# A two-direction state-space scan: half of the state sum by an accumulating transfer, row squares in four column groups

## Chip, cores and metric

The kernel runs on one core of a Trainium2 chip. The metric is the time of one execution on the device, in microseconds (us); lower is better. TensorE does the matmuls, VectorE and ScalarE the elementwise work, POOL (GpSimd) some elementwise work and the transfers that add into their destination, SP (SyncE) the plain transfers.

## What is computed

Tokens are looked up in a table, a two-direction Mamba block is added, then an attention block and a mixture of experts. Only the Mamba block is touched. Cut to what matters:

```
def step(h, ins):
    dt_t, B_t, C_t, u_t = ins
    dA = exp(dt_t[..., None] * A)
    h = dA * h + (dt_t * u_t)[..., None] * B_t[:, None, :]
    return h, einsum('bdn,bn->bd', h, C_t)
...
dt = softplus(x_dbl[..., :DT_RANK] @ Wdt.T + bdt)
y = (scan(step) + uc * Dp) * silu(z)
out = layernorm(y @ Wout.T)             # once forward, once on the reversed rows
combined = concat([fo, bo]) @ Wfuse.T + bfuse
```

32 sequences of 512 rows with 256 channels; inside, 512 channels and 32 states.

## The kernel before

One call, `mamba_stage`, walks through 64 **slots**: for each sequence s a forward one (d = 0) and a reverse one (d = 1), t = 2 s + d. Channels lie on partitions, in four tiles of 128, each 512 rows long; work on two tiles at once (128x1024) is called a half. Five engines run loops written by hand (each `slots`), in a fixed order, tied together by semaphores. A slot finishes the scan of t and at the same time prepares t + 1, and it carries the layer norm and the fusion of t - 1.

VectorE, in order: `conv` of t + 1 (L834), `dead_part` (L899, the states that have decayed, into qq), `scan` (L889, the live state, into tp), in the reverse slot `ln_stats`, `bc_product` (L842), `outputs` (L904: tp times C, 128x2048 in one operation), `more_states` (a branch that is not taken here), in the forward slot `xt_low` (L821), `sums` (L942: tp plus qq, two halves), `gate` (L951: tp times silu(z) into yz, two halves), `dead_test` (L851, L853), `softplus` of t + 1 (L874 and L877 for each half), `dead_mask`, `softplus_end` (L882, writes v, from which the next slot's scan inputs and decays start).

ScalarE, ahead of softplus: v (L448), abs (L457), in the forward slot `xt_copy` (L410), exp, sum (L474), `row_var` (L396, the mean square of a row of t - 1, plus eps), log (L480), `finish` (L510: the fused rows scaled into fb), then `last_tap_and_bias` (L420) for the next convolution and the decays (L485).

TensorE: z projection of t + 1 (L641; waits for the convolution), x_dbl (L650), first half of the fusion (L712), dt projection (L659), second half, `row_squares` (L701: the squares as weights, a column of ones moving, eight matmuls, two records each), u projection (L641), `dead_sums` (L666) in the middle of it, `dead_count`, `out_proj` of t (L690; waits for finish on ScalarE, whose PSUM it overwrites, and for the gate), `state_sum` (L682) in the middle of that.

POOL: `add_input` (L337, transfers that add uc times D into qq), `add_rows` (L316, transfers that add fb into the result), forward `add_bias` (L305), reverse `ln_scale` (L285 to L290), `row_scale` (L297: the root that finish waits for), forward `gather` of sequence s + 2 (L274, L277, four indirect transfers), `scan_inputs` (L322, L328).

Of the kernel before, what the change touches and what calls it, by code (L numbers as in the profile page):

```python
# [56 lines left out]
def mamba_stage(nc, tok_ids, table, w, h1_dram):  # L57
# [6 lines left out]
    with ctx:  # L64
# [3 lines left out]
        def sem(name):  # L68
# [55 lines left out]
        r2 = sb("r2", [P, TT])  # L124
        r3 = sb("r3", [P, TT])
# [19 lines left out]
          d0_ok dt_ok dtu_ok tp_ok da_ok h_ok hc_ok q_ok du_ok mix0 mix1 yv_ok yz_ok xm_ok qd_ps gt_ok ct_ok cnt_ps  # L145
          fl_ok s_ps o_ps fo_ok sq_ok ss_ps rv_ok rr_ok f_ps fin_ok h1_st acc gt2 e_bc e_da e_tp e_h e_hc e_y""".split()
# [44 lines left out]
        def _(sp):  # L191
# [3 lines left out]
            def broadcast(t, d):  # L195

                if not (isinstance(t, int) and t < 2):
                    wait_apart(sp, S["hc_ok"], t - 1)
# [10 lines left out]
            def more_states(t, d):  # L209
# [3 lines left out]
                with sp.If(go > 0):  # L213
                    with sp.Fori(1, NS) as n:
                        c = sp.snap(sp_count)
                        if not (isinstance(t, int) and t == 0):
                            sp.wait_ge(S["hc_ok"], t)
# [31 lines left out]
        def _(pool):  # L249
# [31 lines left out]
            def ln_scale(s):  # L281
                wait_apart(pool, S["st_ok"], s + 1)
# [57 lines left out]

            gather(0)
# [6 lines left out]
            def slots(s, first):  # L348
                for d in range(DIRS):
                    t = 2 * s + d  # L350
                    add_input(t, d)
                    if not first:
                        add_rows(t - 2, d, s - 1)
                    if d == 0:
                        add_bias(s + 1)
                    else:
                        ln_scale(s + 2)
                    if not (first and d == 0):
                        row_scale(t - 1)
                    if d == 0:  # L360
                        gather(s + 2)
                    scan_inputs(t + 1, 1 - d)
# [13 lines left out]
        def _(act):  # L376
# [117 lines left out]
            def project_copies(t, parts):  # L494

                for k in parts:
# [3 lines left out]
                    act.activation(fo[:, k, :], po[k][:], ACT.Copy).then_inc(S["fo_ok"], 1)  # L500
# [73 lines left out]
            def slots(s, first):  # L574
                for d in range(DIRS):
# [7 lines left out]
                    softplus_exp(t + 1, (0,))  # L583
                    softplus_abs(t + 1, (1,))
# [14 lines left out]
            project_copies(2 * NSEQ - 1, range(KD))  # L599
            row_var(2 * NSEQ - 1)  # L600
# [4 lines left out]
        def _(pe):  # L605
# [88 lines left out]
            def row_squares(t, last=False):  # L694
# [4 lines left out]
                for j in range(TT):  # L699
                    for k in range(KD):  # L700
                        i = mm(pss[:, j:j + 1], sq[:, k, j * P:(j + 1) * P], ones[:, 0:1],  # L701
                               start=(k == 0), stop=(k == KD - 1))
                i.then_inc(S["ss_ps"], 1)

            def fusion(t, d, halves=range(2)):
                pe.wait_ge(S["fo_ok"], KD * (t + 1))
# [9 lines left out]
            def front(t, d, s_next, turn, back):  # L716
# [17 lines left out]
                in_proj(t + 1, 1 - d, 0, range(2))  # L734
                dead_sums(t, d)
# [25 lines left out]
            row_squares(2 * NSEQ - 1, True)  # L761


        @block.vector
        def _(dve):
# [39 lines left out]
            def ln_stats(s):  # L805
# [5 lines left out]
                i.then_inc(S["gt2"], 1)  # L811
                wait_apart(dve, S["gt2"], s + 1)
# [55 lines left out]
            def softplus(t):  # L868


                for h, mm in pairs():
# [65 lines left out]
            def sums(t):  # L937

                for h, mm in pairs():
                    dve.wait_ge(S["hc_ok"], t + 1)  # L940
                    dve.wait_ge(S[f"mix{h}"], 16 * (t + 1))
                    tt(tp[:, mm, :], tp[:, mm, :], qq[:, mm, :], ALU.add).then_inc(S["yv_ok"], 1)  # L942

            def gate(t, d):

                if not (isinstance(t, int) and t == 0):
                    dve.wait_ge(S["o_ps"], KD * t)
                dve.wait_ge(S["z_ok"], MD * (t + 1))
                for h, mm in pairs():
                    dve.wait_ge(S["yv_ok"], NP * t + h + 1)  # L950
# [1360 lines left out]
```

## Time and profile before

| | us |
|---|---|
| median of 3 runs | 3888.03 (3886.52 to 3889.06) |
| the profiled execution | 3887.42 |
| its span, first to last instruction | 3885.9 |
| the Mamba stage within it, roughly | 0 to 2200 |

| engine | busy us | share of the span |
|---|---|---|
| TensorE | 3666.1 | 94% |
| VectorE | 3356.2 | 86% |
| ScalarE | 2940.4 | 76% |
| POOL | 2417.7 | 62% |

The shares are means over three stages. For this change only the Mamba stage counts, and in it the timeline of one pair of slots: what each engine waits for, and how long before it is wanted each result is ready.

### The profile page before, as it was taken

To read this page: it belongs to the slowest core of one execution; us is meant where nothing else is said; L and a number is where in the kernel's file an instruction comes from. 1 tells how busy PE (TensorE), PEld (TensorE's weight loads), DVE (VectorE), ACT (ScalarE), POOL (GpSimd) and SP (SyncE) were. 2 spreads that over 40 slices of the span, in tenths; PEclk is the share of its full clock that TensorE was granted. 3 is DMA by queue.
4 is the path that set the end of the run, shared out by engine and by line. 5 is a ranking of instruction groups with operands and counts; after the bars stand their busy time and mean duration, and the time that the engine had idled before them with its cause. 6 is when DMAs were issued, how large, how long until landed. Compare 5 with 4: busy or idle time off the path is not lost. (4 is left out here: it accounts for less than half of the span.)

```text
span 3885.9 us, 70521 instructions
## 1 busy us (share of the span) xinstructions
PE 3666.1 (94%) x19212; PEld 2676.2 (69%) x19213; DVE 3356.2 (86%) x6582; ACT 2940.4 (76%) x4862; POOL 2417.7 (62%) x2145
## 2 busy tenths in 40 slices
PE   5999999999999999999999699999996899999998
PEld 3666666666666666666666377777775788888887
DVE  6999999999999999999999489998996566666665
ACT  5899999999999999999999577777774444444444
POOL 3556566666666666666565657877776455555555
PEclk8999999999999999999999899999997999999999
DMA  4444454445454545455555322222222555555555
GB/s 109 82 88 91 88 92 89 91 88 92 90 96 90 96 90 94 92 92 94 89 90 90 81 69 91 94 95 91 95 91 104 114 96 96 95 94 98 86 97 84
DMA packets 235375, 358.07 MB, mean 92 GB/s; under 512 B 25985, under 2 KB 163586, under 8 KB 235266
## 3 DMA queue, kind: packets, MB, share of 16 engines
q0 software_dynamic: 130288, 215.02, 32.2%
q1 hardware_dynamic: 101536, 139.53, 13.5%
q10 hardware_dynamic: 3442, 2.21, 0.2%
q8 instruction: 51, 0.84, 0.1%
q14 instruction: 58, 0.48, 0.0%
HBM read 121.07 MB, written 168.49 MB: 75 GB/s over the span
## 5 line engine op out<-in xcount | busy, mean ns | idle before, releaser
L641 PE MATMUL pj<-xt,win 128*128 128x512 f32 x3144 | 828.4, 413 | 31.7 <-DVE uc L834 24.7
L641 PEld LDWEIGHTS pj<-xt,win 128*128 128x128 f32 x3144 | 584.2, 190 | 222.6 <-DVE uc L834 55.7
L2037 POOL DMA_INDIRECT out<-e_y,e_to x272 | 470.8, 1731 | 367.9 <-ACT e_y L2143 308.2
L834 DVE SCALAR_TENSOR_TENSOR uc<-pj,convw,uc 128x511 f32<-128x511 f32 (+2 forms) x780 | 516.8, 728 | 5.7 <-ACT uc L420 5.7
L690 PE MATMUL po<-yz,wout 128*128 128x512 f32 x1024 | 473.3, 605 | 39.0 <-ACT fb L510 39.0
L322 POOL TENSOR_TENSOR wk<-v,uc 128x512 f32<-128x512 f32 x260 | 325.6, 1285 | 281.2 <-DVE v L882 280.4
L2088 PE MATMUL e_p<-e_w,e_a 128*128 128x256 f32 x3264 | 416.2, 284 | 0.8 <-DVE e_a L2198 0.8
L2088 PEld LDWEIGHTS e_p<-e_w,e_a 128*128 128x128 f32 x3264 | 393.7, 188 | 11.1 <-DVE e_a L2198 2.3
L2076 PE MATMUL e_p<-e_xt,e_w 128*128 128x512 f32 x1632 | 395.2, 397 | 4.1 <-DVE e_xt L2190 2.4
L690 PEld LDWEIGHTS po<-yz,wout 128*128 128x128 f32 x1024 | 184.0, 189 | 276.5 <-issue 275.8
L2076 PEld LDWEIGHTS e_p<-e_xt,e_w 128*128 128x128 f32 x1632 | 303.2, 189 | 74.9 <-issue 5.8
L2196 DVE CAST e_a<-e_af 128x512 fp32r<-128x512 f32 x272 | 118.6, 436 | 254.1 <-ACT e_af L2136 250.4
L328 POOL TENSOR_TENSOR tp<-wk,bb 128x512 f32<-128x512 f32 x260 | 327.5, 1290 | 0.0
L297 POOL TENSOR_TENSOR r<-r,neg_half 128x4 f32<-128x4 f32 x64 | 100.8, 1575 | 355.6 <-ACT r L396 355.6
L1309 POOL DMA_INDIRECT expert_in<-a_xs,a_idx x256 | 252.8, 988 | 98.5 <-issue 89.2
L889 DVE TENSOR_TENSOR_SCAN tp<-y,tp 128x512 f32<-128x512 f32 x256 | 308.0, 1258 | 0.0
L2136 ACT ACTIVATE e_af<-e_p 128x512 f32<-128x512 f32 x272 | 162.2, 599 | 188.4 <-PE e_p L2076 186.8
L2143 ACT ACTIVATE e_y<-e_p,e_share 128x256 f32<-128x256 f32 x272 | 114.3, 471 | 241.2 <-PE e_p L2088 241.2
L277 POOL DMA_INDIRECT g<-in_table,idc x136 | 217.5, 1599 | 59.6 <-issue 31.1
L712 PE MATMUL po<-wfus,fo 128*128 128x256 f32 x1024 | 246.7, 384 | 3.3 <-ACT sq L501 3.3
L712 PEld LDWEIGHTS po<-wfus,fo 128*128 128x128 f32 x1024 | 190.5, 191 | 79.6 <-issue 55.2
L650 PE MATMUL px<-uc,wx 128*112 128x512 f32 x520 | 244.1, 592 | 0.0
(244 smaller groups left out, 8540.0 us busy)
## 6 DMA issues: line engine op xcount, KB each, us to landing
qq<-uc POOLq DMA_DIRECT2D x128, 512.0 KB, 5.5
e_x<-expert_in SPq DMA_DIRECT2D x138, 260.0 KB, 2.6
bb<-bc SPq DMA_DIRECT2D x65, 512.0 KB, 5.7
h_rows<-fb POOLq DMA_DIRECT2D x64, 512.0 KB, 10.8
h_rows<-g SPq DMA_DIRECT2D x34, 512.0 KB, 5.9
h_rows<-cvec POOLq DMA_DIRECT2D x33, 512.0 KB, 12.2
a_h<-h_rows SPq DMA_DIRECT2D x128, 128.0 KB
out<-a_bs SPq DMA_DIRECT2D x128, 128.0 KB
```

The lines of the kernel that those rows point to most:

```text
L322: pool.tensor_tensor(wk[:, m, :], v[:, m, :], uc[d][:, m, :], ALU.mult).then_inc(S["dtu_ok"], 1)
L328: pool.tensor_tensor(tp[:, m, :], wk[:, m, :], bb[d][:, 0, :], ALU.mult).then_inc(S["tp_ok"], 1)
L641: i = mm(pj[m][:], win[d][wp][:, k, c:c + P], xt[xp][:, k, :], start=(k == 0 and n == 0), stop=(k == KD - 1 and n == 2))
L650: i = mm(px[0:NXR, :], wx[d][:, m, :], uc[d][:, m, :], start=(m == 0), stop=(m == MD - 1))
L690: i = mm(po[k][:], wout[d][:, m, k * P:(k + 1) * P], yz[:, m, :], start=(m == 0), stop=(m == MD - 1))
L712: i = mm(po[h][:, jj * DM:(jj + 1) * DM], fo[:, k, j * P:(j + 1) * P], wfus[d][:, k, :], start=(k == 0), stop=(k == KD - 1))
L834: stt(uc[d][:, m, to], pj[m][:, of], convw[d][:, m, tap:tap + 1], uc[d][:, m, to], ALU.mult, ALU.add).then_inc(S["cv"], 1)
L889: nc.vector.tensor_tensor_scan(tp[:, m, step], y[:, m, step], tp[:, m, step], 0.0, ALU.mult, ALU.add).then_inc(S["h_ok"], 1)
L1309: pool.indirect_dma_start(out=xd_dram, out_offset=bass.IndirectOffsetOnAxis(ap=idx[:, k, j:j + 1].bitcast(U32), axis=0), in_=xs[c % SENDS] ...
L2037: pool.indirect_dma_start(out=out, out_offset=bass.IndirectOffsetOnAxis(ap=to[n][:, j:j + 1].bitcast(U32), axis=0), in_=y[n][:, j, :], in_ ...
L2076: o = mm(p1[m][:], w1[i][wp][:, k, m * P:(m + 1) * P], xt[xp][:, k, :], start=(k == 0 and s == 0), stop=(k == KD - 1 and s == 2))
L2088: o = mm(p2[n][:, j, :], a[ap][:, m, (n * HT + j) * P:(n * HT + j + 1) * P], w2[i][wp][:, m, :], start=(m == 0 and s == 0), stop=(m == MF ...
```

## The change

It has two parts, and work on POOL is put in another order.

**State sum.** The first half of tp + qq stays on VectorE. The second is a transfer from POOL's queue that adds qq to tp (`add_states`). `outputs` works in two halves, the second half first, so that the transfer can be issued after it; a nop after `more_states` tells POOL that qq is final. `gate` is cut in two: the first half at its old place, the second between the halves of `softplus`, where it waits for the transfer. In POOL's slot `add_states` comes right after `add_input`; `gather` (forward) and `ln_scale` (reverse) follow, then `row_scale`, then `add_rows` and `add_bias`.

**Row squares.** Ones are now the weights (128x32) and the squares move (128x128): each of the four row tiles writes its sums to 32 partitions of its own. ScalarE copies the 128x128 result out with scale and eps (`row_mean`, between exp of the first half and abs of the second), TensorE transposes it (`turn_squares`, between the halves of the u projection), and `row_var` picks one column for each row tile.

Elsewhere semaphores are merged and keep the same waits (in the attention stage too), and fusion loses one wait that another implied.

```
+            def add_states(t):
+                wait_apart(pool, S["hc_ok"], NP * t + 1)
+                wait_apart(pool, S["ms_ok"], t + 1)
+                wait_apart(pool, S["mix1"], 16 * (t + 1))
+                pool.wait_ge(S["c_tab"], 1)
+                pool.dma_start(tp[:, 2:MD, :].rearrange("p m n -> p (m n)"),
+                               qq[:, 2:MD, :].rearrange("p m n -> p (m n)"), accum_op=ALU.add
+                               ).then_inc(S["summed"], 16)
...
@@ ACT
             def row_var(t):
-                act.wait_ge(S["ss_ps"], t + 1)
+                act.wait_ge(S["rt_ps"], t + 1)
...
-                act.activation(r2[:], pss[:, 0:TT], ACT.Identity, bias=eps[:], scale=1.0 / DM).then_inc(S["rv_ok"], 1)
+                act.activation(r2[:], pss[:, P:2 * P:P // TT], ACT.Copy).then_inc(S["rv_ok"], 1)
+            def row_mean(t):
+                act.wait_ge(S["ss_ps"], t + 1)
+                act.activation(rows2[:], pss[:, 0:P], ACT.Identity, bias=eps[:], scale=1.0 / DM).then_inc(S["rc_ok"], 1)
...
@@ PE
-                for j in range(TT):
-                    for k in range(KD):
-                        i = mm(pss[:, j:j + 1], sq[:, k, j * P:(j + 1) * P], ones[:, 0:1],
+                group = P // TT
+                for k in range(KD):
+                    for j in range(TT):
+                        i = mm(pss[j * group:(j + 1) * group, 0:P], ones[:, 0:group], sq[:, k, j * P:(j + 1) * P],
                                start=(k == 0), stop=(k == KD - 1))
                 i.then_inc(S["ss_ps"], 1)
+            def turn_squares(t):
+                pe.wait_ge(S["rc_ok"], t + 1)
+                nc.tensor.transpose(pss[:, P:2 * P], rows2[:], ident[:]).then_inc(S["rt_ps"], 1)
...
                 in_proj(t + 1, 1 - d, 0, range(2))
+                if back > 1:
+                    turn_squares(t - 2)
                 dead_sums(t, d)
...
@@ DVE, outputs, sums, gate
-                tt(tp[:], tp[:], bb[d][:, 1, :].unsqueeze(1).to_broadcast([P, MD, SEQ]), ALU.mult
-                   ).then_inc(S["hc_ok"], 1)
+                for h, mm in reversed(pairs()):
+                    tt(tp[:, mm, :], tp[:, mm, :], over_pair(bb[d][:, 1, :]), ALU.mult).then_inc(S["hc_ok"], 1)
...
-                    tt(tp[:, mm, :], tp[:, mm, :], qq[:, mm, :], ALU.add).then_inc(S["yv_ok"], 1)
+                tt(tp[:, 0:2, :], tp[:, 0:2, :], qq[:, 0:2, :], ALU.add).then_inc(S["yv_ok"], 1)
...
+                    dve.wait_ge(S["yv_ok"], t + 1)
+                else:
+                    dve.wait_ge(S["summed"], 16 * (t + 1))
```

The order on three engines, at the places that the prediction speaks of. **POOL, forward slot, before**, from `add_rows` to `gather` (r is the row scale; ISA and REGISTER_ALU rows are waits and their registers):

```order
L316 DMA h_rows<-fb 128x4x256
L154 ISA
L305 ISA
L305 DMA h_rows<-cvec 128x4x256
L297 TENSOR_TENSOR r<-r,neg_half 128x4
L271 REGISTER_ALU
L272 REGISTER_ALU
L274 ISA
L274 COPY idc<-ids 128x4
L154 REGISTER_ALU
L277 DMA g<-in_table,idc 128x256 x4
L320 REGISTER_ALU
```

The same slot **after**, from `add_states` (L348) on:

```order
L348 DMA tp<-qq 128x1024
L272 ISA
L273 REGISTER_ALU
L274 REGISTER_ALU
L275 ISA
L275 COPY idc<-ids 128x4
L155 REGISTER_ALU
L278 DMA g<-in_table,idc 128x256 x4
L297 ISA
L298 TENSOR_TENSOR r<-r,neg_half 128x4
```

`row_scale` (L297 before, L298 after) stood ahead of `gather` and now stands behind it; the new transfer is ahead of both, `add_rows` and `add_bias` follow.

**VectorE before**, from the sums to the first half of softplus, with the semaphores that each waits for:

```order
L942 TENSOR_TENSOR tp<-tp,qq 128x1024 [waits m_mix0,m_hc_ok]
L942 TENSOR_TENSOR tp<-tp,qq 128x1024 [waits m_mix1,m_hc_ok]
L951 TENSOR_TENSOR yz<-tp,zs 128x1024 [waits m_yv_ok,m_z_ok]
L951 TENSOR_TENSOR yz<-tp,zs 128x1024 [waits m_yv_ok]
L851 TENSOR_TENSOR dgt<-alb,px 128x4 [waits m_cnt_ps,m_qd_ps]
```

The same stretch **after**, to the second half of softplus:

```order
L970 TENSOR_TENSOR tp<-tp,qq 128x1024 [waits m_mix0,m_hc_ok]
L982 TENSOR_TENSOR yz<-tp,zs 128x1024 [waits m_yv_ok,m_z_ok]
L879 TENSOR_TENSOR dgt<-alb,px 128x4 [waits m_cnt_ps,m_qd_ps]
L881 SCALAR_TENSOR_TENSOR dgt<-dgt,alok 128x4 [waits m_gt_ok]
L903 SCALAR_TENSOR_TENSOR wk<-wk,lg 128x1024 [waits m_l_ok,m_w_ok]
L906 TENSOR_TENSOR wk<-y,wk 128x1024 [waits m_g_ok]
L982 TENSOR_TENSOR yz<-tp,zs 128x1024 [waits m_summed]
L903 SCALAR_TENSOR_TENSOR wk<-wk,lg 128x1024 [waits m_l_ok,m_w_ok]
```

Ahead of softplus stand one sum and one half of the gate fewer; the other half of the gate stands behind its first half, with a wait for the transfer.

**ScalarE before**, from exp of the first half to finish:

```order
L465 ACTIVATE y<-lg 128x1024 [waits m_h_ok,m_vc_ok]
L457 ACTIVATE lg<-v 128x1024 [waits m_g_ok,m_v_ok]
L474 ACTIVATE wk<-y 128x1024 [waits m_q_ok,m_tp_ok,m_y_ok]
L465 ACTIVATE y<-lg 128x1024 [waits m_h_ok,m_vc_ok]
L396 ACTIVATE r<-pss,eps 128x4 [waits m_ss_ps]
L480 ACTIVATE lg<-wk 128x1024 [waits m_w_ok]
```

The same stretch **after**:

```order
L482 ACTIVATE y<-lg 128x1024 [waits m_h_ok,m_vc_ok]
L413 ACTIVATE rows<-pss,eps 128x128 [waits m_ss_ps]
L474 ACTIVATE lg<-v 128x1024 [waits m_g_ok,m_v_ok]
L491 ACTIVATE wk<-y 128x1024 [waits m_q_ok,m_tp_ok,m_y_ok]
L482 ACTIVATE y<-lg 128x1024 [waits m_h_ok,m_vc_ok]
L408 ACTIVATE r<-pss 128x4 [waits m_rt_ps]
L497 ACTIVATE lg<-wk 128x1024 [waits m_w_ok]
```

`row_mean` (L413) is new there, and `row_var` (L408) waits for the transpose instead of the squares.

## Rows read from the trace of the kernel before

**Rows 1.** Busy time by stretches; columns: stretch, length, busy (instructions) by engine.

```profile
1000.00:2000.00 1000.00, 974.18 (x3887) 626.17 (x3886) 977.11 (x1211) 914.86 (x1427) 622.13 (x517) 1.00 0.50 91
```

**Rows 2.** Timeline of VectorE, forward slot: start us, length us, instruction, [idle before].

```profile
1059.09 7.95 DVE L834 SCALAR_TENSOR_TENSOR uc<-pj,convw,uc 128x511 f32<-128x511 f32 x12
...
1075.35 2.29 DVE L904 TENSOR_TENSOR tp<-tp,bb 128x2048 f32<-128x2048 f32 x1
1078.43 1.29 DVE L821 TENSOR_TENSOR xt<-pj,xt 128x512 fp32r<-128x512 f32 x2 [0.79 <-ACT xt L410]
...
1081.90 2.35 DVE L951 TENSOR_TENSOR yz<-tp,zs 128x1024 f32<-128x1024 f32 x2
...
1084.44 1.23 DVE L874 SCALAR_TENSOR_TENSOR wk<-wk,lg 128x1024 f32<-128x1024 f32 x1
...
1091.76 0.73 DVE L834 SCALAR_TENSOR_TENSOR uc<-pj,convw,uc 128x511 f32<-128x511 f32 x1
```

**Rows 3.** The same, reverse slot.

```profile
1025.80 7.95 DVE L834 SCALAR_TENSOR_TENSOR uc<-pj,convw,uc 128x511 f32<-128x511 f32 x12
...
1044.41 2.29 DVE L904 TENSOR_TENSOR tp<-tp,bb 128x2048 f32<-128x2048 f32 x1
1046.83 2.36 DVE L942 TENSOR_TENSOR tp<-tp,qq 128x1024 f32<-128x1024 f32 x2
...
1051.77 1.22 DVE L874 SCALAR_TENSOR_TENSOR wk<-wk,lg 128x1024 f32<-128x1024 f32 x1
```

**Rows 4.** Timeline of ScalarE: log of the reverse slot, then the forward slot.

```profile
1048.94 1.04 ACT L480 ACTIVATE lg<-wk 128x1024 f32<-128x1024 f32 x1
...
1082.53 0.29 ACT L396 ACTIVATE r<-pss,eps 128x4 f32<-128x4 f32 x1
1082.68 1.09 ACT L480 ACTIVATE lg<-wk 128x1024 f32<-128x1024 f32 x1
...
1085.71 1.55 ACT L510 ACTIVATE fb<-po,r 128x256 f32<-128x256 f32 x4
```

**Rows 5.** Timeline of TensorE, both slots.

```profile
1021.45 3.69 PE L690 MATMUL po<-yz,wout 128*128 128x512 f32 x8 [0.58 <-ACT fb L510]
1025.07 1.12 PE L682 MATMUL pss<-bcp,smask 32*128 32x512 f32 x2
1026.12 3.70 PE L690 MATMUL po<-yz,wout 128*128 128x512 f32 x8
1029.26 3.31 PE L641 MATMUL pj<-xt,win 128*128 128x512 f32 x12
...
1062.50 3.03 PE L641 MATMUL pj<-xt,win 128*128 128x512 f32 x12 [0.51 <-DVE uc L834]
...
1078.09 1.84 PE L701 MATMUL pss<-ones,sq 128*128 128x1 f32 x16
...
1082.73 1.05 PE L666 MATMUL px<-xmax,wdta 16*128 16x1 f32 x8
...
1087.39 3.69 PE L690 MATMUL po<-yz,wout 128*128 128x512 f32 x8 [0.55 <-ACT fb L510]
```

**Rows 6.** Timeline of POOL, forward slot: row scale, index copy, gathers.

```profile
1082.91 1.10 POOL L297 TENSOR_TENSOR r<-r,neg_half 128x4 f32<-128x4 f32 x1 [9.00 <-ACT r L396]
1083.98 0.32 POOL L274 COPY idc<-ids 128x4 int32 x1
1085.14 1.53 POOL L277 DMA_INDIRECT g<-in_table,idc  x1 [0.84 <-POOL idc L274]
...
1089.23 0.95 POOL L277 DMA_INDIRECT g<-in_table,idc  x1 [0.30 <-issue]
1090.48 2.17 POOL L277 DMA_INDIRECT g<-in_table,idc  x1 [0.30 <-issue]
```

**Rows 7.** Writers of qq, 1000 to 2000: durations in ns, then us to landing.

```profile
L337 POOL DMA_DIRECT2D qq<-uc x62: 834/901/1304, 1003.2 to 1993.4; - x62
...
DMA to landing us min/median/max: 4.6/6.2/8.0
```

More of the change, by code:

```diff
@@ L124, in mamba_stage @@
         r2 = sb("r2", [P, TT])
+        rows2 = sb("rows2", [P, P])
         r3 = sb("r3", [P, TT])
@@ L197, in broadcast @@
                 if not (isinstance(t, int) and t < 2):
-                    wait_apart(sp, S["hc_ok"], t - 1)
+                    wait_apart(sp, S["hc_ok"], NP * (t - 1))
                 wait_apart(sp, S["xd_ok"], t + 1)
@@ L281, in ln_scale @@
             def ln_scale(s):
-                wait_apart(pool, S["st_ok"], s + 1)
+                wait_apart(pool, S["st_ok"], 2 * s + 2)
                 if not (isinstance(s, int) and s == 0):
@@ L351, in slots @@
                     add_input(t, d)
+                    add_states(t)
+                    if d == 0:
+                        gather(s + 2)
+                    else:
+                        ln_scale(s + 2)
+                    if not (first and d == 0):
+                        row_scale(t - 1)
                     if not first:
@@ L355, in slots @@
                         add_bias(s + 1)
[L356 to L361, printed above, removed]
                     scan_inputs(t + 1, 1 - d)
@@ L583, in slots @@
                     softplus_exp(t + 1, (0,))
+                    if not (first and d == 0):
+                        row_mean(t - 1)
                     softplus_abs(t + 1, (1,))
@@ L599, in _ @@
             project_copies(2 * NSEQ - 1, range(KD))
+            row_mean(2 * NSEQ - 1)
             row_var(2 * NSEQ - 1)
@@ L761, in _ @@
             row_squares(2 * NSEQ - 1, True)
+            turn_squares(2 * NSEQ - 1)
         @block.vector
@@ L810, in ln_stats @@
                     i = nc.vector.bn_stats(stats[:, j, :], g[:, j, :])
-                i.then_inc(S["gt2"], 1)
-                wait_apart(dve, S["gt2"], s + 1)
+                i.then_inc(S["st_ok"], 1)
+                wait_apart(dve, S["st_ok"], 2 * s + 1)
                 for j in range(TT):
@@ L866, in over_pair, with softplus @@
                 return row.unsqueeze(1).to_broadcast([P, 2, SEQ])
-            def softplus(t):
-                for h, mm in pairs():
+            def softplus(t, halves=range(NP)):
+                for h in halves:
+                    mm = slice(2 * h, 2 * h + 2)
                     dve.wait_ge(S["w_ok"], NP * t + h + 1)
@@ L937, in sums, with gate @@
             def sums(t):
-                for h, mm in pairs():
-                    dve.wait_ge(S["hc_ok"], t + 1)
-                    dve.wait_ge(S[f"mix{h}"], 16 * (t + 1))
-                    tt(tp[:, mm, :], tp[:, mm, :], qq[:, mm, :], ALU.add).then_inc(S["yv_ok"], 1)
[L944 to L950, printed above, removed]
-                    tt(yz[:, mm, :], tp[:, mm, :], zs[d][:, mm, :], ALU.mult).then_inc(S["yz_ok"], 1)
+                dve.wait_ge(S["hc_ok"], NP * (t + 1))
+                dve.wait_ge(S["mix0"], 16 * (t + 1))
+                tt(tp[:, 0:2, :], tp[:, 0:2, :], qq[:, 0:2, :], ALU.add).then_inc(S["yv_ok"], 1)
+            def gate(t, d, h):
+                if h == 0:
+                    if not (isinstance(t, int) and t == 0):
+                        dve.wait_ge(S["o_ps"], KD * t)
+                    dve.wait_ge(S["z_ok"], MD * (t + 1))
+                    dve.wait_ge(S["yv_ok"], t + 1)
+                else:
+                    dve.wait_ge(S["summed"], 16 * (t + 1))
+                mm = slice(2 * h, 2 * h + 2)
+                tt(yz[:, mm, :], tp[:, mm, :], zs[d][:, mm, :], ALU.mult).then_inc(S["yz_ok"], 1)
             dve_count = dve.alloc_register("dve_states")
@@ L983, in slots @@
                     more_states(t, d)
+                    dve.nop().then_inc(S["ms_ok"], 1)
                     if d == 0:
@@ L986, in slots @@
                     sums(t)
-                    gate(t, d)
+                    gate(t, d, 0)
                     dead_test(t + 1, 1 - d)
-                    softplus(t + 1)
+                    softplus(t + 1, (0,))
+                    gate(t, d, 1)
+                    softplus(t + 1, (1,))
                     dead_mask(t + 1, 1 - d)
@@ L1704, in less_max @@
                     dve.wait_ge(S["s_ps"], 4 * c + n + 1)
-                    nc.vector.tensor_reduce(mx[:, 4 * i:4 * i + 4, :], each, AX_X, ALU.max).then_inc(S["mx_ok"], 1)
-                    dve.wait_ge(S["mx_ok"], 4 * c + n + 1)
+                    nc.vector.tensor_reduce(mx[:, 4 * i:4 * i + 4, :], each, AX_X, ALU.max).then_inc(S["red"], 1)
+                    dve.wait_ge(S["red"], 8 * c + n + 1)
                     after(dve, "pt_ps", 4 * c)
@@ L1722, in add_projection @@
                 dve.wait_ge(S["core_ok"], TT * (c + 1))
-                dve.wait_ge(S["step_ok"], c + 1)
+                dve.wait_ge(S["root_ok"], 2 * c + 2)
                 for n, i in enumerate((1, 0)):
```

21 lines of the change are left out of this document (10 added, 11 removed).

## The prediction

> **What bounds the kernel now.** I read the busy table by stretches first, then the timeline of one pair of slots engine by engine, then the landing time of the state-sum transfers. The change touches only the Mamba stage, which runs 64 slots, a forward one (d = 0) and a reverse one (d = 1) for each of 32 sequences. In the thousand microseconds from 1000 on, VectorE is busy 97.7% and TensorE 97.4% [rows 1], so neither table nor share says which of them sets the pace. The timeline does. Call the start of the convolution (L834) the start of a slot: the forward slot runs from 1059.09 to 1091.76, which is 32.67 us [rows 2], and the reverse slot from 1025.80 to 1059.09, which is 33.29 us [rows 2, 3]. A pair takes 65.96 us, and the pairs after it read alike. Below, times within a slot are counted from its start.
>
> VectorE is the pacemaker: within a pair it stands idle once, 0.79 us before xt_low [rows 2]. But behind it runs a second loop that is nearly as long: convolution, z projection on TensorE, x_dbl, dt projection, then on ScalarE v, abs, exp, sum, log, and back into softplus on VectorE. The reader is to compare when ScalarE has finished the first half's log with when VectorE takes it. Forward: log ends at 1082.68 + 1.09 = 1083.77, taken at 1084.44, a slack of 0.67 us [rows 2, 4]. Reverse: 1048.94 + 1.04 = 1049.98, taken at 1051.77, a slack of 1.79 us [rows 3, 4]. In the same place of the forward slot the dead sums on TensorE end at 1082.73 + 1.05 = 1083.78 [rows 5], and the dead test, which stands just ahead of softplus, needs them. TensorE itself waits at two points: for finish on ScalarE (0.55 us before out_proj) and for the convolution (0.51 us before the forward z projection, none before the reverse one) [rows 5].
>
> **The change part by part.**
>
> *VectorE.* One of two state sums goes: 2.36 / 2 = 1.18 us a slot [rows 3]. The product with C in two halves instead of one, a nop, and sums and gate of one half now standing directly behind one another add what no row shows; the gap between the outputs (1044.41, 2.29 long) and the sums (1046.83) is 0.13 us [rows 3], so I take 0.25 for all, between 0.1 and 0.4. One gate half, 2.35 / 2 = 1.18 us [rows 2], moves from ahead of softplus to between its halves. So VectorE reaches softplus 1.18 + 1.18 - 0.25 = 2.1 us earlier, but from there to the next slot it needs 7.32 us as before (1091.76 - 1084.44) plus 1.18, that is 8.50.
>
> That makes the slack above the deciding number. A slot gets shorter only if softplus can start more than 1.18 us earlier than now.
>
> *ScalarE and TensorE ahead of softplus.* row_mean, 128x128 out of PSUM, is new on ScalarE ahead of the log. The nearest rows are the 128x4 one, which takes 0.15 until the next starts, and fb, 128x256, at (1087.26 - 1085.71) / 4 = 0.39 [rows 4]; I take 0.25. Row squares keep 16 records. They took 1.84 us [rows 5]; if the four column groups run side by side they take a quarter, 0.46, and if switching to column groups holds TensorE up they take more. The nearest row to a switch is that into the 32-row product L682: it starts 3.62 us after eight out_proj records, where L641 starts 3.14 after the same eight [rows 5], so 0.48 for each switch, 2.8 us with two. I take 1.84. The turn of the rows is one short TensorE record, 0.13 by the dead sums' 1.05 / 8 [rows 5]. row_var must now wait for it: forward it is reached at 23.44 + 0.25 = 23.69, the turn is done at about 23.64 + 0.13 and a signal later, near 23.95, so 0.25 us of waiting; in the reverse slot under 0.1.
> The Trainium skill (TensorEngine Tiling, Key Properties) says that changing the tiling mode drains TensorE, while tiles of one mode work in parallel; the rows on L682 agree with a cost of that kind, and no row yet shows column groups. By its parallel tiles alone row squares would be near 0.46 us, by its drain they would lie above 1.84; the sum below stands at 1.84 without it.
>
> Forward slot: log 24.68 + 0.25 + 0.25 = 25.2; dead sums 24.69 + 0.13 + 0.26 for the test = 25.1; VectorE is there at 23.2. Softplus starts at 25.2 instead of 25.35, and the slot lasts 25.2 + 8.5 = 33.7 us, **1.03 longer**. Reverse slot: 24.18 + 0.25 + 0.07 = 24.5 instead of 25.97; with the second gate half fed in time that gives 33.0 us, 0.29 shorter.
>
> *The transfer.* It can be issued once both products and the nop are done, in the reverse slot at 18.61 + 2.42 + 0.1 = 21.1. The nearest rows are the sister transfers qq<-uc: landing after 6.2 us, 4.6 to 8.0 [rows 7]. So 27.3 (25.7 to 29.1), against the gate's second half at 24.5 + 2.4 = 26.9: a wait of 0.4 us (0 to 2.2), 33.4 us in all. In the forward slot the gate comes at 27.6 and the sum at 18.7 + 6.2 = 24.9: no wait.
>
> *POOL's queue.* In the forward slot add_states now stands at 18.85, and gather behind it goes ahead of row_scale; before, row_scale ran at 23.82 and gather after it, from 24.89 to 33.56 [rows 6]. finish on ScalarE needs row_scale, out_proj on TensorE needs finish. New order: issue 0.90 [rows 7] to 19.75, the index copy to 20.07, 0.84 to 20.91. A gather takes 0.95 by itself (the third); the first ran 1.53 because it ended 1.00 after the softplus operation that was already running (1084.44 + 1.23) [rows 2, 6]. Laid against VectorE's new order: the first waits out the sum and ends at 22.7, the second after 0.30 at 24.0, the third at 25.25, the fourth waits out softplus and ends at 27.3; row_scale waits out the next softplus operation, 27.6, and ends 28.6. As an undivided block (8.67 us, then 1.10) it would be 29.5. ScalarE is ready at 26.62 + 0.25 = 26.9, so finish starts 1.7 us late (0 to 2.6). It ends at 30.15, out_proj starts at 30.3, and the reverse slot's z projection 7.81 us later [rows 5] at 38.1. The convolution would allow it at 33.7 + 3.46 = 37.2. TensorE is therefore 0.93 us late (1.8 as a block) through the whole reverse slot; that covers the transfer's wait, and softplus starts at 24.5 + 0.93: 33.9 us, **0.64 longer** than 33.29. At its end out_proj has 0.2 us to spare before the next convolution, so nothing more is carried over.
>
> Sum: 1.03 + 0.64 = 1.67 us a pair, 32 pairs, 53 us. The profiled execution took 3887.4 us in all (span 3885.9), 0.6 under the median of the runs: 3887.4 + 53 = **3941 us**. What TensorE may gain in row squares and VectorE in the sum stands in front of waits and is worth nothing there.
>
> **The rivals.**
>
> *Faster.* VectorE stays the pacemaker. It then saves 1.18 - 0.25 = 0.93 us a slot, 64 slots, 60 us: 3828. This decides from the point at which softplus may start at 24.2 in the forward slot (25.35 - 1.18). Against it: ScalarE has no gap between v and log, so log at 24.7 would have to come 0.5 us earlier while row_mean is added. For it: the reverse slot alone does pass that point. Chance 0.09.
>
> *No change.* Gather lands in VectorE's waits and ends before 26; row squares are quick; the sum lands early: forward 0.7 longer, reverse 0.4 shorter, 0.3 x 32 = 10 us, 3897, the edge of what a measurement can tell from none (0.2%, 8 us). A little under it 0.08; from 3897 to 3920, 0.15.
>
> *Slow row squares, or groups that don't run side by side.* At 2.8 us the dead sums come 0.96 later: forward softplus at 26.0, the slot 1.9 longer; reverse 0.7 to 1.6 longer; 83 to 112 us, 3970 to 3999. Chance 0.13.
>
> *Gather held throughout.* If each gather takes the longest row, 2.17 + 0.30 [rows 6], row_scale ends at 31.9, TensorE is 4.2 us late, the pair 5.0 longer: 3887 + 159 = 4046. Chance 0.06.
> The Trainium skill (SBUF — State Buffer, section on the two separate sides) calls the port pair of VectorE and GpSimd an exclusive lock, held for the whole instruction; the stretched gather agrees. By it this rival would come about if VectorE were never idle there.
>
> **Numbers.** My forecast has 0.49 (3920 to 3970), the others as given. Faster by over 0.2% 0.09, within 0.2% 0.08, slower 0.83. The range 3893 to 4005 leaves out the faster case, the held gather and half of no change.
>
> **What would show it.** Right: VectorE idle ahead of the first softplus operation, about 2 us forward and 1.5 reverse, put down to the log or the dead sums; ScalarE idle 1.5 to 2.5 us before fb in the forward slot, put down to row_scale; TensorE's out_proj waiting there; no wait for the sum's transfer worth naming. Wrong: softplus starting without a wait, or fb on time, or row squares well off 1.84 us with the slot following them.

## The result, and the profile after

The changed kernel takes 3956.99 us (median of 4 runs, 3954.52 to 3957.25), the kernel before 3887.28 beside it: a ratio of 1.0179 (95% interval 1.0167 to 1.0192), 69.7 us longer. The forecast was 3941, within 3893 to 4005. Sign and size hold, but two terms behind them were wrong, in opposite directions, so that hitting the range is in part luck.

A slot runs, as before, from one start of the convolution to the next (L834 before, L862 after). Over 26 pairs in the middle of the stage:

| | forward slot, median | reverse slot, median | pair, mean |
|---|---|---|---|
| before | 32.67 | 33.27 | 65.94 |
| forecast | 33.7 | 33.9 | 67.6 |
| after | 35.08 | 33.13 | 68.23 |

Busy time of the thousand microseconds from 1000 on, kernel after, as in [rows 1] (stretch, length, busy time of TensorE, weight loads, VectorE, ScalarE and GpSimd, granted clock, DMA share, GB/s):

```profile
1000.00:2000.00 1000.00, 938.47 (x3793) 574.12 (x3792) 911.28 (x1173) 895.76 (x1407) 587.54 (x527) 0.97 0.54 104
```

VectorE has fallen from 977 to 911, TensorE from 974 to 938, and the granted clock, 1.00 before, is 0.97: somewhere in here TensorE ran at its lower level. Timeline of VectorE, kernel after, a reverse slot and the forward one behind it, to be held against [rows 3] and [rows 2] (start us, length us, instruction, idle before and what ended it):

```profile
1534.19 7.95 DVE L862 SCALAR_TENSOR_TENSOR uc<-pj,convw,uc 128x511 f32<-128x511 f32 x12
...
1558.30 1.23 DVE L903 SCALAR_TENSOR_TENSOR wk<-wk,lg 128x1024 f32<-128x1024 f32 x1 [0.61 <-ACT lg L497]
...
1561.18 1.23 DVE L982 TENSOR_TENSOR yz<-tp,zs 128x1024 f32<-128x1024 f32 x1 [0.36 <-DMA tp<-qq]
...
1567.24 7.95 DVE L862 SCALAR_TENSOR_TENSOR uc<-pj,convw,uc 128x511 f32<-128x511 f32 x12
...
1588.15 1.29 DVE L849 TENSOR_TENSOR xt<-pj,xt 128x512 fp32r<-128x512 f32 x2 [2.17 <-ACT xt L427]
...
1593.65 0.16 DVE L879 TENSOR_TENSOR dgt<-alb,px 128x4 f32<-128x4 f32 x1 [1.73 <-PE px L686]
...
1593.93 1.22 DVE L903 SCALAR_TENSOR_TENSOR wk<-wk,lg 128x1024 f32<-128x1024 f32 x1
...
1602.38 2.70 DVE L862 SCALAR_TENSOR_TENSOR uc<-pj,convw,uc 128x511 f32<-128x511 f32 x4
```

In the reverse slot softplus starts 24.11 us in, and waits for the log. In the forward slot VectorE waits 2.17 us and then 1.73 us, and softplus starts 26.69 us in, 1.5 later than forecast. What made it late stands on TensorE, at the end of the reverse slot. Its timeline, same kernel, against [rows 5]:

```profile
1552.31 0.65 PE L722 MATMUL pss<-sq,ones 128*32 128x128 f32 x16
1552.88 3.02 PE L661 MATMUL pj<-xt,win 128*128 128x512 f32 x12
...
1559.77 0.28 PE L693 MATMUL px<-dgt,ones 128*128 128x4 f32 x2
1562.42 5.39 PE L710 MATMUL po<-yz,wout 128*128 128x512 f32 x8 [2.37 <-DVE yz L982]
...
1568.79 3.70 PE L710 MATMUL po<-yz,wout 128*128 128x512 f32 x8
1571.93 3.32 PE L661 MATMUL pj<-xt,win 128*128 128x512 f32 x12
```

Eight out_proj records take 5.39 us, where the same eight took 3.69 before [rows 5] and the next eight take 3.70. Busy time and clock of the stretch, cut at these rows (columns as above; TensorE's busy time comes first, the granted clock after GpSimd's):

```profile
1552.90:1560.00 7.10, 7.10 (x39) 5.81 (x35) 6.12 (x8) 7.04 (x10) 5.70 (x6) 1.00 0.84 216
1560.00:1562.42 2.42, 0.05 (x1) 0.01 (x1) 2.06 (x3) 1.93 (x6) 1.85 (x2) 1.00 0.08 15
1562.42:1567.80 5.38, 5.38 (x9) 2.08 (x9) 5.31 (x7) 4.95 (x9) 0.40 (x1) 0.68 0.74 97
1567.80:1571.90 4.10, 4.10 (x10) 1.67 (x10) 4.10 (x8) 4.07 (x7) 4.10 (x4) 1.00 0.00 0
```

TensorE is fully busy at clock 1.00, does almost nothing for 2.42 us, and comes back at a mean of 0.68, that is, for the greater part at the lower of its two levels (1.2 of 2.4 GHz); then the clock is full again. The z projection of the forward slot therefore starts at 1571.93, 4.69 us into the slot. In the reverse slot, which no such stretch precedes, it starts 3.41 us in. Everything behind it, from x_dbl to the log and the dead sums, comes 1.3 us late.

What TensorE waits for are two results that end almost together: the gate's second half at 1562.41 (1561.18 + 1.23, VectorE's timeline above), which waits for the transfer, and fb on ScalarE at 1562.29, which waits for the row scale:

```profile
1560.72 1.57 ACT L527 ACTIVATE fb<-po,r 128x256 f32<-128x256 f32 x4 [0.49 <-POOL r L298]
```

On GpSimd, against [rows 6], the order forecast did come, but not its length. Timeline, kernel after, forward slot:

```profile
1587.57 1.09 POOL L278 DMA_INDIRECT g<-in_table,idc  x1 [0.84 <-POOL idc L275]
...
1591.70 1.05 POOL L278 DMA_INDIRECT g<-in_table,idc  x1 [0.30 <-issue]
1593.02 1.04 POOL L298 TENSOR_TENSOR r<-r,neg_half 128x4 f32<-128x4 f32 x1 [0.27 <-ACT r L408]
```

The four gathers of this slot take 1.00 to 1.13 each, and the row scale is done 26.8 us into the slot, not 28.6. Over the thousand microseconds from 1000 on the waits of the changed kernel that matter here are these (who waits for whom: us in total, times, longest):

```profile
PE po L710 <- ACT fb L527: 35.5, 24, 2.4
DVE xt L849 <- ACT xt L427: 31.8, 15, 2.2
...
DVE dgt L879 <- PE px L686: 24.0, 14, 1.7
...
ACT fb L527 <- POOL r L298: 8.5, 18, 0.5
...
DVE yz L982 <- DMA tp<-qq: 5.5, 12, 1.2
```

### The profile page after: what moved, and what is told of

The parts are those of the page before. It is cut to its first block and busy times, and to the rows that moved or that the text cites. A ratio compares the mean times of both kernels' runs of the same rounds, so it can differ in the third digit from the quotient of the medians.

```text
span 3955.8 us, 70904 instructions
## 1 busy us (share of the span) xinstructions
PE 3656.0 (92%) x19276; PEld 2605.5 (66%) x19277; DVE 3286.2 (83%) x6582; ACT 2965.0 (75%) x4926; POOL 2401.2 (61%) x2209
## 5 line engine op out<-in xcount | busy, mean ns | idle before, releaser
L710 PE MATMUL po<-yz,wout 128*128 128x512 f32 x1024 | 524.0, 659 | 102.1 <-ACT fb L527 83.3
L862 DVE SCALAR_TENSOR_TENSOR uc<-pj,convw,uc 128x511 f32<-128x511 f32 (+2 forms) x780 | 516.8, 728 | 4.9 <-ACT uc L437 4.9
L710 PEld LDWEIGHTS po<-yz,wout 128*128 128x128 f32 x1024 | 201.7, 207 | 372.6 <-issue 329.9
L348 POOL DMA_DIRECT2D tp<-qq x64 | 54.6, 854 | 442.0 <-DVE tp L934 349.7
L918 DVE TENSOR_TENSOR_SCAN tp<-y,tp 128x512 f32<-128x512 f32 x256 | 291.1, 1190 | 0.0
L502 ACT ACTIVATE y<-v,amat 128x512 f32<-128x512 f32 x260 | 166.5, 711 | 98.0 <-DVE v L911 97.9
```

The lines of the kernel that those rows point to most:

```text
L710: i = mm(po[k][:], wout[d][:, m, k * P:(k + 1) * P], yz[:, m, :], start=(m == 0), stop=(m == MD - 1))
L862: stt(uc[d][:, m, to], pj[m][:, of], convw[d][:, m, tap:tap + 1], uc[d][:, m, to], ALU.mult, ALU.add).then_inc(S["cv"], 1)
L918: nc.vector.tensor_tensor_scan(tp[:, m, step], y[:, m, step], tp[:, m, step], 0.0, ALU.mult, ALU.add).then_inc(S["h_ok"], 1)
```

## Experiments

Four theories stood against one another. **A:** TensorE's idle stretch ahead of the reverse out_proj lets its clock fall, and the forward slot starts late. **B:** the gate's second half, now behind the start of softplus, is all of it. **C:** GpSimd's order holds up the row scale, and with it fb and out_proj. **D**, formed after the second run: what counts on GpSimd is when the last gather ends, since the inputs of the scan stand behind it.

**The state sum without the new row squares.** The changed kernel with the old row squares put back, and row_mean and the turn taken out:

```diff
-                for k in range(KD):
-                    for j in range(TT):
-                        i = mm(pss[j * group:(j + 1) * group, 0:P], ones[:, 0:group], sq[:, k, j * P:(j + 1) * P],
+                for j in range(TT):
+                    for k in range(KD):
+                        i = mm(pss[:, j:j + 1], sq[:, k, j * P:(j + 1) * P], ones[:, 0:1],
```

> The changed kernel with the row squares as they were (squares as weights, no copy, no transpose); the new way of the sum stays whole. Theory A (clock): in the reverse slot TensorE reaches out_proj 1.2 us later again, so its idle stretch ahead of it is near 1.2 us instead of 2.37, the granted clock stays at 1.00, out_proj takes 3.7 us instead of 5.39, the forward slot's z projection starts at 3.4 and not at 4.7, and the forward slot lasts 33.5 to 33.9 us instead of 35.05: 3905 to 3920 us. Theory B (place of the gate's second half alone): the forward slot stays near 35, 3945 to 3957 us. Theory C (POOL's order): ScalarE still waits 0.5 us for the row scale and the time stays within 10 us of 3957.

3914.87 us, ratio 1.0071 (1.0054 to 1.0087); slots 33.77 and 32.80, a pair 66.80 in the mean. Timeline of TensorE in this kernel, reverse slot into forward slot, which starts at 1539.80:

```profile
1535.43 3.69 PE L701 MATMUL po<-yz,wout 128*128 128x512 f32 x8 [1.36 <-ACT fb L521]
...
1543.24 3.33 PE L652 MATMUL pj<-xt,win 128*128 128x512 f32 x12
```

The idle stretch is 1.36 us, out_proj has its 3.69 (granted clock 1.00), the z projection starts 3.44 us in, and softplus 25.33 us in, all as A says. C said that the time would stay near 3957, but it fell by 42 us although fb still waits for the row scale, 0.57 us in most reverse slots and, in the forward slot, this (ScalarE):

```profile
1567.43 1.57 ACT L521 ACTIVATE fb<-po,r 128x256 f32<-128x256 f32 x4 [0.58 <-POOL r L297]
```

Comparing a reverse slot from each kernel: out_proj starts 28.23 us in with the change and 28.42 here, but TensorE is through with the work ahead of it at 25.86 with the change and at 27.06 here. The quick row squares (0.65 us for 1.84) bought TensorE nothing but a longer wait.

**The row squares without the state sum.** The kernel before, with the lines of the diff above exchanged the other way, and row_mean, the turn and a few merged semaphores as in the change.

> The kernel before with the row squares in column groups (and copy and transpose) alone; sum, gate and POOL's order as before. VectorE sets the pace there with 0.67 and 1.79 us of slack at softplus, and TensorE gains about 1 us a slot, which it stands idle ahead of out_proj: 1.7 to 1.9 us instead of 0.55 to 0.68. Theory A: if the clock holds over that, 3884 to 3892 us, no change; if it falls there as well, out_proj takes up to 1.7 us more in each slot and 3915 to 3950 us. Theories B and C: 3884 to 3892 us, whatever TensorE idles.

3923.91 us, 1.0095 (1.0078 to 1.0112); slots 32.68 and 34.52. The time lies in the range that A gave for a falling clock, but by accident: none of the three theories had the cause. The clock does fall here, in 11 of 26 reverse slots, behind two short idle stretches (TensorE, granted clock 0.68 over the second row):

```profile
1202.88 0.38 PE L682 MATMUL px<-dgt,ones 128*128 128x4 f32 x2 [0.96 <-DVE dgt L870]
1203.81 5.39 PE L699 MATMUL po<-yz,wout 128*128 128x512 f32 x8 [0.55 <-ACT fb L516]
```

The forward slot behind such a place lasts 32.81 us, behind one whose clock held 32.68; that is 0.06 us a pair. The loss is the 1.25 us of the reverse slot, which lasts 34.52 us either way. GpSimd's timeline from the end of a forward slot (the reverse one starts at 1041.12), then VectorE's:

```profile
1032.57 1.94 POOL L298 TENSOR_TENSOR r<-r,neg_half 128x4 f32<-128x4 f32 x1 [9.43 <-ACT r L397]
...
1042.32 0.95 POOL L278 DMA_INDIRECT g<-in_table,idc  x1 [0.30 <-issue]
1043.30 5.04 POOL L323 TENSOR_TENSOR wk<-v,uc 128x512 f32<-128x512 f32 x4
1048.30 5.01 POOL L329 TENSOR_TENSOR tp<-wk,bb 128x512 f32<-128x512 f32 x4
```

```profile
1051.39 6.36 DVE L906 TENSOR_TENSOR_SCAN tp<-y,tp 128x512 f32<-128x512 f32 x4
...
1085.92 4.55 DVE L906 TENSOR_TENSOR_SCAN tp<-y,tp 128x512 f32<-128x512 f32 x4
```

The row scale starts 0.4 us later in its slot and takes 1.94 us instead of 1.10 [rows 6], the gathers move back, and the last ends 2.15 us into the reverse slot. Before it ended 0.89 in (1090.48 + 2.17 [rows 6], less 1091.76 [rows 2]). The scan's inputs start 1.26 later, and the reverse scan takes 6.36 us. In the kernel before, the two scans read:

```profile
1036.06 5.11 DVE L889 TENSOR_TENSOR_SCAN tp<-y,tp 128x512 f32<-128x512 f32 x4
...
1069.35 4.55 DVE L889 TENSOR_TENSOR_SCAN tp<-y,tp 128x512 f32<-128x512 f32 x4
```

So already before, the reverse scan was 0.56 us longer than the forward one. The records of the reverse scan (shortest, median and longest in ns), before and here, and GpSimd's last products ahead of the scan, before:

```profile
L889 DVE TENSOR_TENSOR_SCAN tp<-y,tp x4: 1192/1194/1761, 1036.1 to 1040.0; 128x512 f32<-128x512 f32 x4
...
L906 DVE TENSOR_TENSOR_SCAN tp<-y,tp x4: 1192/1193/3011, 1051.4 to 1056.6; 128x512 f32<-128x512 f32 x4
...
1031.71 5.04 POOL L328 TENSOR_TENSOR tp<-wk,bb 128x512 f32<-128x512 f32 x4
```

One record of the four, the first, has all of the difference. It is no wait for its input: the product for its tile had ended 3.1 us before it began (1.8 in this kernel). It ends 1.08 or 1.09 us behind the last of GpSimd's four products, in all 26 reverse slots of either kernel: VectorE is held within the instruction while GpSimd multiplies, and that time counts as busy. My reading that VectorE stands idle once in a pair had passed over it. From it theory D.

**Gather alone moved.** The kernel before, with nothing but the gather ahead of add_rows and the row scale:

```diff
                     add_input(t, d)
+                    if d == 0:
+                        gather(s + 2)
                     if not first:
                         add_rows(t - 2, d, s - 1)
...
                         row_scale(t - 1)
-                    if d == 0:
-                        gather(s + 2)
```

> The kernel before with gather ahead of add_rows, add_bias and the row scale in POOL's forward slot, nothing else. What the run of the row squares alone showed (theory D): a gather that ends late holds up POOL's scan inputs and with them VectorE's scan in the reverse slot, 5.1 us there against 4.55 in the forward one. Theory D: the scan takes 4.55 us in both slots, 0.55 us a pair, 3866 to 3876 us. If POOL's queue doesn't count in the kernel before: 3884 to 3891 us.

3869.93 us, ratio 0.9957 (0.9944 to 0.9971), as D said. Both scans now take 4.55, and the reverse slot 32.73 instead of 33.27: 0.54 a pair against the 0.56 of the scan.

**More work for TensorE.** The changed kernel, with the row squares computed three times over:

```diff
-                for k in range(KD):
+                for k in [k for again in range(3) for k in range(KD)]:
                     for j in range(TT):
```

> The changed kernel with the row squares' eight matmuls done three times over: 1.2 to 1.3 us more work on TensorE in every slot, with the same result. Theory A: the work fills the idle stretch ahead of out_proj (2.37 us to 1.1), the clock holds, and the kernel with more work is faster than the changed one: 3905 to 3930 us. Theories B and C: as slow as the changed one or slower, since dead sums and the row copy come later: 3955 to 3990 us.

3918.09 us (3912.24 to 3922.40), 39 us less than the changed kernel, with 32 more TensorE records in each slot. The timeline of TensorE in this kernel, end of a reverse slot:

```profile
1593.15 1.52 PE L722 MATMUL pss<-sq,ones 128*32 128x128 f32 x48
...
1603.26 3.69 PE L710 MATMUL po<-yz,wout 128*128 128x512 f32 x8 [1.49 <-ACT fb L527]
```

The idle stretch is mostly 1.36 to 1.49 us in the reverse slot and 1.25 in the forward one, eight records take 3.69, and a pair takes 66.85, 1.38 less than after. Under B the added work could only be neutral or cost; A alone has it shorten the time.

**Twice.** The same with `range(2)`:

> The changed kernel with the row squares' matmuls done twice, 0.4 to 0.6 us more work on TensorE in each slot; the same result. Idle stretch ahead of the reverse out_proj 1.8 to 1.9 us, between 2.37 (clock falls) and 1.49 with three times (clock holds). Theory A: if the clock holds at 1.00, 3912 to 3922 us as with three times; if it falls in a part of the slots, in between, 3925 to 3950; the time follows the number of slow out_proj, not the work. Theory B: 3955 to 3970 us.

3949.48 us (3928.70 to 3951.62), 1.0144 (1.0115 to 1.0172), where A has it for a clock that falls in a part of the slots. The idle stretch of the reverse slot is 1.8 to 1.9 us, and 22 of 26 forward slots are long. Out_proj in two reverse slots of the same kernel behind equal waits, the second with the clock down (0.68); the forward slots behind them last 33.56 and 34.71 us:

```profile
1011.13 3.69 PE L710 MATMUL po<-yz,wout 128*128 128x512 f32 x8 [1.77 <-ACT fb L527]
...
1078.05 5.39 PE L710 MATMUL po<-yz,wout 128*128 128x512 f32 x8 [1.77 <-ACT fb L527]
```

**State sum ahead of out_proj.** In the changed kernel, state_sum fills some of the stretch:

```diff
+                state_sum(t)
                 if back > 0:
                     out_proj(t - 1, 1 - d, range(1))
-                state_sum(t)
```

> The changed kernel with the state sum (L702, 1.05 us) ahead of out_proj on TensorE instead of in its middle; nothing else. It fills the idle stretch and takes 1.05 us out of the way from finish to the z projection. Theory A: idle 1.3 us, granted clock 1.00, z at 3.4 in both slots, 3905 to 3920 us. Theory B: softplus in the forward slot is bound by log and dead sums alone, 3945 to 3957 us.

3925.92 us (3918.85 to 3926.51), ratio 1.0095 (1.0078 to 1.0112): 31 us less than the changed kernel, but 6 above the most that A allowed. The idle stretch is 1.3 us, yet the clock still fell in 12 of 26 reverse slots: sixteen records in one piece took 7.13 us in one slot and 8.66 in another. The edit also takes 1.05 us out of the way from out_proj to the z projection, which in most slots starts 3.41 us in even where the clock fell; so this run can't tell what the clock alone is worth.

**Without the transfer and the second half of the state sum.**

```diff
-                    add_states(t)
...
-                    dve.wait_ge(S["summed"], 16 * (t + 1))
+                    pass
```

> The changed kernel without the second half of the state sum: neither the transfer nor anything in its place, and the gate's second half waits for nothing (that half of the output lacks the decayed states and uc times D). In the changed kernel POOL reaches the row scale late because the transfer ahead of it waits for the product on VectorE, ScalarE waits 0.5 us for it, and the gate 0.4 us for the landing. Without both, TensorE's idle stretch ahead of the reverse out_proj is 1.4 to 1.9 us instead of 2.37. Theory A (clock): the granted clock holds, out_proj takes 3.7 us, forward slot 33.7, 3908 to 3922 us; what is left above 3887 is the place of the gate's second half. If the transfer's own cost were only the two waits: 0.4 us a pair, 3940 to 3948 us.

3897.30 us (8 runs, 3896.16 to 3899.49), 1.0027 (1.0016 to 1.0038), lower than A's range. With nothing to land, TensorE's wait is 1.76 us, not 2.37, and the clock falls in 17 of 26 pairs. Two outcomes of one wait, from TensorE's timeline:

```profile
1538.61 5.39 PE L709 MATMUL po<-yz,wout 128*128 128x512 f32 x8 [1.76 <-ACT fb L526]
...
1606.19 3.70 PE L709 MATMUL po<-yz,wout 128*128 128x512 f32 x8 [1.76 <-ACT fb L526]
```

The forward slot behind the first is 35.01 us long, that behind the second 33.55; the reverse slot is 32.57 in both cases, the granted clock 0.68 over the first row and 1.00 over the second. One kernel, one execution, the same wait: this is the comparison that shows the clock's price, 1.46 us. A pair whose clock held is 66.12, 0.18 over before: that is what the whole change costs without the transfer and without the clock (forward 0.88 more, reverse 0.70 less). The transfer, with its issue in GpSimd's queue, adds the rest in two ways: it lengthens the reverse slot (33.13 against 32.57), and it puts 0.6 us on TensorE's idle stretch, after which the clock fell every time.

**The row scale ahead of the gathers.** The changed kernel, with row_scale put directly behind add_states:

```diff
                     add_states(t)
+                    if not (first and d == 0):
+                        row_scale(t - 1)
                     if d == 0:
                         gather(s + 2)
                     else:
                         ln_scale(s + 2)
-                    if not (first and d == 0):
-                        row_scale(t - 1)
```

> The changed kernel with the row scale ahead of gather (forward) and of ln_scale (reverse) in POOL's order, right behind the transfer. ScalarE no longer waits 0.5 us for it in the reverse slot, so TensorE's idle stretch ahead of out_proj is 1.9 us instead of 2.37. Theory A (clock): if the granted clock holds at 1.00 over that, the forward slot falls from 35.05 to 33.8 us and the time to 3912 to 3925; if it still falls, 3940 to 3957. Theory C (POOL's order by itself): half a microsecond in one slot of two, 3938 to 3945 us, whatever the clock does.

4067.93 us, 1.0454 (1.0428 to 1.0481), the opposite of what was expected, and the end of C in the form in which I held it. GpSimd, then ScalarE, then TensorE, in one reverse slot of this kernel:

```profile
1560.58 0.86 POOL L348 DMA_DIRECT2D tp<-qq  x1 [9.65 <-DMA qq<-uc]
1561.15 2.20 POOL L298 TENSOR_TENSOR r<-r,neg_half 128x4 f32<-128x4 f32 x1
```

```profile
1563.52 1.57 ACT L527 ACTIVATE fb<-po,r 128x256 f32<-128x256 f32 x4 [3.92 <-POOL r L298]
```

```profile
1565.22 5.59 PE L710 MATMUL po<-yz,wout 128*128 128x512 f32 x8 [4.74 <-ACT fb L527]
```

In the forward slot the gathers and, behind them, the two transfers to h_rows now stand last and run into the reverse slot (D); its scan inputs start at 1536.13, 2.6 us into it, where the kernel before has 0.9, and the scan takes 7.6 us. The transfers to qq and the sum that waits for them come late; the row scale stands in the queue behind the sum's issue; fb waits 3.92 us for it and out_proj 4.74. Of these two orders on GpSimd only the change's keeps the accumulating transfer affordable.

**A version that beats both.** Taken from the first experiment (old row squares): the half that goes by transfer is half 0, scanned first and sent while the other half is scanned; both gate halves stand ahead of softplus again; state_sum stands ahead of out_proj, which takes tiles 2, 3, 0, 1. The gathers stay ahead of the row scale. The order on VectorE alone:

```diff
-                    scan(t, d)
+                    scan(t, d, 0)
+                    outputs(t, d, 0)
+                    scan(t, d, 1)
+                    more_states(t, d)
+                    dve.nop().then_inc(S["ms_ok"], 1)
...
+                    gate(t, d, 1)
                     gate(t, d, 0)
...
-                    softplus(t + 1, (0,))
-                    gate(t, d, 1)
-                    softplus(t + 1, (1,))
+                    softplus(t + 1)
```

> The transfer kept, but made to fit: scan of tiles 0 and 1, their product with C, scan of tiles 2 and 3, the branch, and then the transfer of the first half can be issued, 2.5 us (forward) and 5 us (reverse) earlier; both halves of the gate stand ahead of softplus as in the kernel before; state sum ahead of out_proj; row squares as before. Theory A with the place of the gate: VectorE reaches softplus 0.9 us earlier than in the kernel before and nothing follows it that was not there, log and dead sums (24.7 to 25.0) allow it: forward 32.2 to 32.4 us, reverse 32.2 to 32.6, 3840 to 3860 us. If the transfer itself costs the time (contention, its landing), 3890 us or more.

3837.20 us, ratio 0.9870 (0.9855 to 0.9885); slots 32.31 and 32.02. From 1000 to 2000 it reads

```profile
1000.00:2000.00 1000.00, 992.36 (x3974) 642.66 (x3974) 967.88 (x1248) 937.38 (x1462) 594.98 (x557) 1.00 0.57 110
```

The transfer lands 5.6 us after its issue (5.1 to 6.1), nobody waits for it, and TensorE is busy 99% of the time. Of the 49 us below the kernel before, 16 come also without any transfer, by the gathers' place alone (3869.93 above).

**The same with the new row squares.**

> The same with the row squares in column groups. TensorE has 1 us a slot less to do and idles that much more. Theory A: 3838 to 3860 us if the clock holds at 1.00; 3865 to 3900 us if it falls in one slot of two. If row squares count by their own time, it is faster than the kernel with the old ones.

3840.62 us, 0.9881 (0.9866 to 0.9897): no different within the intervals. From 1000 to 2000:

```profile
1000.00:2000.00 1000.00, 964.69 (x4008) 600.91 (x4006) 966.18 (x1245) 942.26 (x1489) 592.73 (x559) 1.00 0.57 110
```

Here no idle stretch harms the clock, and the quick row squares are still worth nothing. TensorE is busy 965 us instead of 992 in the same time, so its work alone did not set the pace there, full as it was.

## Why the prediction came out as it did

- **Softplus bound by the log and the dead sums, with the gate half added behind it: right.** Where the clock held, the first experiment has softplus at 25.33 and a forward slot of 33.77 (forecast 25.2 and 33.7), and the reverse slot is 32.80 (33.0). In the changed kernel VectorE does wait there, in the reverse slot 0.61 us for the log (I had named 1.5), in the forward one 1.73 for the dead sums (2).
- **GpSimd's order, 0.64 on the reverse slot: wrong.** I laid the gathers against a VectorE that works without pause and let two of the four be stretched. In the slot shown each began while VectorE stood idle or was in the last half microsecond of an instruction, and they took 1.00 to 1.13. Even where the clock held and softplus started when I had said (first experiment), the row scale ended 27.5 us into the slot and not 28.6: fb waited 0.58 us and not 1.7, out_proj was no later than the next convolution allows, and the reverse z projection started 3.41 us in, as without any delay. In the changed kernel fb started without a wait in the forward slot; by my own list that was a sign that the step is wrong. Reverse slot: 33.13, not 33.9. The Trainium skill (SBUF — State Buffer, SBUF: two separate sides) has a lock between the two engines: whichever starts first, a VectorE instruction with two inputs in SBUF or a GpSimd one that reads SBUF, holds it to its end. The row scale of 1.94 us in the second experiment agrees: it began at 1032.57 while the gate ran on VectorE (1031.27 to 1033.62) and ended 0.89 us behind it. So does the scan's first record behind GpSimd's products. The gathers agree by half: they are stretched behind a running VectorE instruction, but in the kernel before the 50 operations of softplus that started during one (300 to 2000 us) took their usual 1.22 us.
- **"Nothing more is carried over": wrong, and the larger error.** TensorE carries 1.28 us (4.69 less 3.41) from the reverse slot into the forward one, since its clock falls after 2.37 us without work. The price is 1.38 us a pair, after against the kernel with thrice the row squares: 44 us by 32 pairs, 39 by the medians. The run without the second sum has 1.46 in one and the same execution. Without the clock's fall the change would cost about 31. My sum had no term for what TensorE's idle time does to TensorE.
- **Row squares at 1.84 us: mis-sized.** They take 0.65. One behind another, sixteen records of 128 columns would take 1.85 us, an estimate from out_proj's eight of 512 (3.69 / 32 x 16). The Trainium skill (TensorEngine Tiling (Array Packing), Key Properties) says that different tiles can work in parallel; the 0.65 agrees. The drain that it gives for a change of mode has no room behind them in this trace: the projection starts 0.57 us after they do. "Worth nothing there" was too kind: the 1.2 us that TensorE saved became idle time, in the reverse slot ahead of out_proj.
- **The transfer: nearly right.** It landed after 7.2 us (6.5 to 8.0) instead of 6.2, and VectorE waited 0.36 for it in the slot shown (forecast 0.4). That I had the wait covered by TensorE's delay was wrong.
- **The small terms: right.** row_mean takes 0.35 to 0.40, 0.24 to the next start (forecast 0.25); the turn 0.27, 0.20 to the next start (0.13).

So the sum of 1.67 us a pair stood against 2.29: forward 1.03 against 2.41, of which the clock is 1.3 to 1.5; reverse 0.64 against a gain of 0.14. Two errors, of about 0.8 and 1.4, partly cancelled; that the time came within 16 us of the forecast is luck to that extent. The two halves of the change, each alone, cost 28 and 37 us, which nearly add up to 70, but that is no account of it: the 37 come almost wholly from late gathers, which the whole change has moved.

What stays open is what decides the clock at an idle stretch of middle length. From 500 to 2500 us, all out_proj rows with over 0.9 us idle ahead of them, and the reverse slots of the second experiment (the clock counted as fallen where eight records took over 4.2 us, or sixteen over 7.5):

| kernel | idle before, us | clock held | clock fell |
|---|---|---|---|
| sum only; squares thrice | 1.2 to 1.5 | 96 | 0 |
| the same | 2.5 | 1 | 3 |
| state sum first | 1.2 to 1.5 | 14 | 13 |
| no second sum | 1.8 | 9 | 17 |
| squares twice | 1.2 to 1.3 | 7 | 0 |
| the same | 1.8 to 2.5 | 3 | 23 |
| after | 1.2 | 6 | 0 |
| the same | 2.2 to 2.4 | 0 | 26 |
| row scale first | 1.9 to 4.8 | 0 | 25 |
| squares only, reverse slots | 0.95 and 0.55, two short records between | 14 | 11 |

The length of the stretch goes with the outcome, but alone it does not fix it: 1.3 us did harm in one kernel and none in another.

## What to carry to other kernels

Ask of every engine that a change makes wait longer what the wait does to that engine afterwards: on TensorE, time saved ahead of a wait can come back as a lower clock on the work behind it, and it is read by the length of the same records before and after. Compare one operation's length across slots (5.11 against 4.55 for the scan): time for which an engine is held within an instruction counts as busy, so it shows there and not as idle time. A transfer that does an engine's work pays if it is issued early enough that the engine's order need not be bent around its landing.

## What the hardware showed that I had not expected

- TensorE did the same eight records in 5.39 instead of 3.69 us, at a mean granted clock of 0.68, after 2.37 us with almost no work, and 39 us of the kernel's time came back when it was given three times the work in front of that wait.
- Sixteen records in four column groups took 0.65 us, against 1.84 for sixteen with a single column of ones.
- The place of one instruction of 1 us in GpSimd's queue made 111 us: 4067.93 against 3956.99.
- A scan record on VectorE took 3.01 us instead of 1.19 while GpSimd's products ran, and ended 1.08 or 1.09 us behind the last of them, in 26 of 26 reverse slots.
